# One-hot rows of the slot table in 16 bits, tile innermost, read by the matrix engine at a step of 32 bytes

## The reference

```
xn = layernorm(x)
Q, K, V = spike(layernorm(xn @ W.T + b) * g + beta >= 1)      # three projections, 16 heads of 16
attn = 16 - hamming(Q, K) + log-distance bias                 # 4096 x 4096, never formed: it is linear in Q, K, V
s = spike(layernorm(spike(attn @ V) @ Wo.T + bo))
ids = argmin over 8 centroids of dist2(rmsnorm(xn), centroid) # one expert for each token
y = gated MLP of expert ids[token], 256 -> 2 x 512 -> 256     # a * silu(g), then down
out = x + s * silu(y + xn)
```

## Time and profile before

| | us |
|---|---|
| median of 3 runs | 391.56 (388.51 to 393.59) |
| the profiled execution | 388.83 |
| its span, first to last instruction | 387.0 |
| PE busy | 364.7 (94%) |
| DVE busy | 315.9 (82%) |
| POOL busy | 234.7 (61%) |
| ACT busy | 224.6 (58%) |

### The profile page before, as it was taken

How to read it: one execution, slowest core, us unless ns; L and a number is a source line. 1 busy time by engine, 2 the same in 40 slices (tenths; PEclk the granted TensorE clock), 3 DMA queues, 4 the chain that set the end, 5 groups by cost and what they waited for, 6 DMA issues and landing times.

```text
span 387.0 us, 9389 instructions
## 1 busy us (share of the span) xinstructions
PE 364.7 (94%) x2583; PEld 307.6 (79%) x2584; DVE 315.9 (82%) x785; ACT 224.6 (58%) x611; POOL 234.7 (61%) x296
## 2 busy tenths in 40 slices
PE   8999999999969999985999999999999999999981
PEld 4878888888848888864888888888888888888871
DVE  5989999997688999997578777887877777777873
ACT  5589789888733333444455555555555555555551
POOL 4688777778601444786466666666666666666642
PEclk9999999999999999999899999999999999999998
DMA  6687768463398021539122222223222233321000
GB/s 212 199 303 204 220 180 285 145 180 98 104 207 222 29 83 41 153 96 307 34 72 87 67 67 71 80 86 95 76 81 82 79 95 89 92 78 55 29 16 0
DMA packets 31874, 45.44 MB, mean 117 GB/s; under 512 B 4113, under 2 KB 25810, under 8 KB 31716
## 3 DMA queue, kind: packets, MB, share of 16 engines
q1 hardware_dynamic: 25200, 29.73, 26.2%
q0 software_dynamic: 6416, 15.26, 13.6%
q10 hardware_dynamic: 228, 0.10, 0.1%
HBM read 36.84 MB, written 15.63 MB: 136 GB/s over the span
## 4 chain that ended last, share of the span: by engine, by line
PE 69%; DVE 9%; DMA 8%; issue 7%; ACT 3%; POOL 2%; ACTq 1%; SPq 1%; DVEq 0%; POOLq 0%
PE bank L632 20%; PE bank L450 16%; PE bank L650 10%; PE bank L511 4%; DMA row_a<-rows_a,slot_id 4%; PE bank L615 3%; PE bank L604 2%; DMA down_sb<-in_down_w 2%; PE bank L554 2%; PE bank L429 2%; PE bank L515 2%; ACT d_hi L825 2%; DVE d_lo L1218 1%; PE bank L523 1%; DVE up_lo L1172 1%
## 5 line engine op out<-in xcount | busy, mean ns | idle before, releaser
L1218 DVE TENSOR_TENSOR d_lo<-down_sb,d_hi 128x1024 fp32r<-128x1024 f32 x39 | 47.8, 1226 | 31.7 <-ACT d_hi L825 30.8
L1366 POOL DMA_INDIRECT row_a<-rows_a,slot_id x39 | 41.3, 1060 | 46.8 <-DVE e_o L1232 30.5
L825 ACT ACTIVATE d_hi<-down_sb 128x1024 fp32r x39 | 41.3, 1060 | 41.7 <-issue 26.3
L1399 POOL DMA_INDIRECT out_x<-e_o,slot_id x39 | 44.3, 1137 | 21.0 <-issue 14.5
L632 PE MATMUL bank<-up_hi,e_xh 128*128 x156 | 52.5, 418 | 0.0
L1372 POOL DMA_INDIRECT row_s<-rows_s,slot_id x39 | 39.7, 1018 | 15.6 <-issue 11.6
L632 PE MATMUL bank<-up_lo,e_xh 128*128 x156 | 48.9, 395 | 0.0
L632 PE MATMUL bank<-up_hi,e_xl 128*128 x156 | 48.6, 392 | 0.0
L807 ACT ACTIVATE e_xh<-bank 128x256 fp32r<-128x256 f32 x39 | 15.0, 384 | 40.9 <-PE bank L604 15.2
L753 ACT ACTIVATE junk<-bank 128x256 bf16<-128x256 f32 x96 | 35.4, 378 | 5.1 <-PE bank L450 4.7
L450 PE MATMUL bank<-w_hi,x_hi 128*128 128x264 f32 (+1 forms) x128 | 35.5, 359 | 0.0
(11 more groups left out here) (221 smaller groups left out, 979.2 us busy)
## 6 DMA issues: line engine op xcount, KB each, us to landing
up_raw<-in_up_w SPq DMA_DIRECT2D x16, 512.0 KB, 4.0
rows_a<-xn SPq DMA_DIRECT2D x32, 129.0 KB, 2.4
rows_a<-in_x SPq DMA_DIRECT2D x8, 512.0 KB, 11.6
down_sb<-in_down_w SPq DMA_DIRECT2D x8, 512.0 KB
xs<-in_x SPq DMA_DIRECT2D x7, 512.0 KB, 4.0
rows_s<-s_out SPq DMA_DIRECT2D x8, 256.0 KB, 2.5
blk_tab<-in_blocks SPq DMA_DIRECT2D x1, 1024.0 KB, 5.7
row_a<-rows_a,slot_id POOLq DMA_INDIRECT x39
```

The source lines that it names most:

```text
L825: act.activation(d_hi[:, :, :], down_sb[:, bass.ds(e, 1), :, :].rearrange("p a c n -> p (a c) n"), ACT.Copy).then_inc(d_high, 1)
L1218: V.tensor_tensor(d_lo[:, :, :], down_sb[:, bass.ds(e, 1), :, :].rearrange("p a c n -> p (a c) n"), d_hi[:, :, :].bitcast(F32), ALU.subtra ...
L1366: G.indirect_dma_start(row_a[s % 4][:, :], None, rows_a, bass.IndirectOffsetOnAxis(ap=slot_id[:, s:s + 1], axis=0), bounds_check=N - 1, oo ...
L1399: G.indirect_dma_start(out, bass.IndirectOffsetOnAxis(ap=slot_id[:, s:s + 1], axis=0), e_o[s % 4][:, :], None, bounds_check=N - 1, oob_is_ ...
```

## The change

Everything about the two one-hot tables is kept in 16 bits, and the index of the tile becomes the innermost one. `low_hot` goes from [128, 16, 128] to [128, 128, 16], `high_hot` from [128, 16, 39] to [128, 39, 16], `high_id` from [128, 16, 2, 39] to [128, 2, 39, 16]. The sizes in bytes are the same.

- POOL writes three new tables in 16 bits, between its stage A and its first `norms_out`: `col_of` (2048 elements in each partition, element (s, n) = s), `tile_of_slot` (39 x 16, element (s, n) = s) and `base16` (32 elements). They lie in the place at `at_set`.
- DVE writes the column of each token as 16 bits (`low16`) in place of 32, and a 16-bit copy of its tile (`high16`), one instruction more. In `slot_one_hots` the same four instructions then have only 16-bit operands in SBUF, all with an innermost step of one element. The comparisons read written-out tables, and the vector of 16 tokens' values is repeated along the outer index instead of the inner one.
- DVE waits for the three tables in `positions` and in `slot_one_hots(0)`. ACT waits for both halves of the one-hots before `high_parts(6)`, since that writes over the tables.
- PE's 32 matmuls stand where they stood, but for tile n they take `low_hot[:, :, n]` and `high_id[:, :, :, n]`: 128 and 78 elements of 2 bytes, each 32 bytes behind the one before.

```diff
--- before.py
+++ after.py
@@ -199,10 +199,14 @@
 
         HT = NT // 2
         assert at_xn[3] + 4 * (D + 2) - at_xn[0] >= 2 * HT * P and at_rs[0] - at_ra[2] >= 2 * HT * P
-        low_hot = [place(f"low_hot{q}", [P, HT, P], BF16, at=at)[0] for q, at in enumerate((at_xn[0], at_ra[2]))]
+        low_hot = [place(f"low_hot{q}", [P, P, HT], BF16, at=at)[0] for q, at in enumerate((at_xn[0], at_ra[2]))]
         at_high = (at_thr, at_ra[2] + 2 * HT * P)
-        high_id = [place(f"high_id{q}", [P, HT, 2, ST], BF16, at=at)[0] for q, at in enumerate(at_high)]
-        high_hot, _ = place("high_hot", [P, HT, ST], BF16, at=at_brow)
+        high_id = [place(f"high_id{q}", [P, 2, ST, HT], BF16, at=at)[0] for q, at in enumerate(at_high)]
+        high_hot, _ = place("high_hot", [P, ST, HT], BF16, at=at_brow)
+        col_of, _ = place("col_of", [P, P, HT], BF16, at=at_set)
+        tile_of_slot, _ = place("tile_of_slot", [P, ST, HT], BF16, at=at_set + 2 * P * HT)
+        base16, low16, high16 = (place(name, [P, NT], BF16, at=at_set + 2 * P * HT + 2 * ST * HT + 2 * NT * n)[0]
+                                 for n, name in enumerate(("base16", "low16", "high16")))
         assert 2 * HT * ST <= 6 * D and 4 * HT * ST <= 12 * D
         assert at_high[1] + 4 * HT * ST <= block_arena[0]
         slot_f, _ = place("slot_f", [P, ST], F32)
@@ -252,6 +256,7 @@
             sem("eye_kept"), sem("sgn_made"), sem("lim_made"), sem("lim_put"), sem("fs_rows"), sem("fs_kept"),
             sem("bo_rows"), sem("lim_n"), sem("sq_cen"), sem("cen_split"))
         cols_set, gain_inv = sem("cols_set"), sem("gain_inv")
+        hot_tables = sem("hot_tables")
         ny_kept, bias_n, pick_set = sem("ny_kept"), sem("bias_n"), sem("pick_set")
         sgn = small[:, 0:8]
         tables_made = sem("tables_made")
@@ -586,8 +591,8 @@
             for q in range(2):
                 pe.wait_ge(slot_hot, q + 1)
                 for n in range(HT):
-                    last = pe.matmul(bank[6][:, 0:2 * ST], low_hot[q][:, n, :],
-                                     high_id[q][:, n, :, :].rearrange("p a s -> p (a s)"),
+                    last = pe.matmul(bank[6][:, 0:2 * ST], low_hot[q][:, :, n],
+                                     high_id[q][:, :, :, n].rearrange("p a s -> p (a s)"),
                                      start=(q == 0 and n == 0), stop=(q == 1 and n == HT - 1))
             last.then_inc(slots_summed, 1)
             for k in range(5, NCH):
@@ -781,6 +786,8 @@
             def high_parts(e):
 
                 for half in range(DC):
+                    if e == E - 2 and half == 0:
+                        act.wait_ge(slot_hot, 2)
                     if e == E - 1:
                         act.wait_ge(at_done, DC * NCH // 2 * (half + 1))
                     act.activation(up_hi[:, e, half, :], up_raw[:, e, half, :], ACT.Copy,
@@ -1121,9 +1128,11 @@
                 step(V.tensor_reduce(rt[:, 2, :], A, AX.X, ALU.add))
                 V.tensor_scalar(rt[:, 0, :], rt[:, 2, :], 1.0 / P, 0.5 / P - 0.5, ALU.mult, ALU.add).then_inc(pos_done, 1)
                 dve.wait_ge(pos_done, 1)
+                dve.wait_ge(hot_tables, 3)
                 step(V.tensor_scalar(rt[:, 0, :], rt[:, 0, :], 12582912.0, None, ALU.add))
                 step(V.tensor_scalar(rt[:, 0, :], rt[:, 0, :], -12582912.0, None, ALU.add))
-                step(V.scalar_tensor_tensor(rt[:, 1, :], rt[:, 0, :], -float(P), rt[:, 2, :], ALU.mult, ALU.add))
+                V.tensor_copy(high16[:, :], rt[:, 0, :])
+                step(V.scalar_tensor_tensor(low16[:, :], rt[:, 0, :], -float(P), rt[:, 2, :], ALU.mult, ALU.add))
 
             def tile_experts():
 
@@ -1135,16 +1144,16 @@
             def slot_one_hots(q):
 
                 ts = slice(q * HT, (q + 1) * HT)
-                over_s = lambda m, n: m.unsqueeze(1).broadcast_to([P, HT, n])
-                per_t = lambda m, n: m.unsqueeze(2).broadcast_to([P, HT, n])
+                over_s = lambda m, n: m[:, ts].unsqueeze(1).broadcast_to([P, n, HT])
                 if q == 0:
                     dve.wait_ge(xt_done, NT)
+                    dve.wait_ge(hot_tables, 3)
                     for k in range(4):
                         dve.wait_ge(row_put[k], 16 * NT // 4)
-                V.tensor_tensor(low_hot[q][:, :, :], over_s(col_no[:, :], P), per_t(rt[:, 1, ts], P), ALU.is_equal)
-                step(V.tensor_tensor(high_hot[:, :, :], over_s(tile_no[:, :], ST), per_t(rt[:, 0, ts], ST), ALU.is_equal))
-                V.tensor_tensor(high_id[q][:, :, 0, :], high_hot[:, :, :], per_t(tile_base[:, ts], ST), ALU.mult)
-                step(V.tensor_scalar(high_id[q][:, :, 1, :], high_hot[:, :, :], row_no[:, 0:1], None, ALU.mult))
+                V.tensor_tensor(low_hot[q][:, :, :], col_of[:, :, :], over_s(low16, P), ALU.is_equal)
+                step(V.tensor_tensor(high_hot[:, :, :], tile_of_slot[:, :, :], over_s(high16, ST), ALU.is_equal))
+                V.tensor_tensor(high_id[q][:, 0, :, :], high_hot[:, :, :], over_s(base16, ST), ALU.mult)
+                step(V.tensor_scalar(high_id[q][:, 1, :, :], high_hot[:, :, :], row_no[:, 0:1], None, ALU.mult))
                 dve.sem_inc(slot_hot, 1)
 
             def slot_ids():
@@ -1349,6 +1358,12 @@
                 step_a(k, 0)
 
 
+            iota = lambda table, pattern, base: G.iota(table, pattern, base=base, channel_multiplier=0,
+                                                       allow_small_or_imprecise_dtypes=True).then_inc(hot_tables, 1)
+            iota(col_of[:, :, :], [[1, P], [0, HT]], 0)
+            iota(tile_of_slot[:, :, :], [[1, ST], [0, HT]], 0)
+            iota(base16[:, :], [[P, NT]], -N)
+
             def norms_out(k, i):
                 c = k + 2 * i
                 for pair in range(2):
```

## The result

| | kernel before | changed kernel |
|---|---|---|
| median | 391.56 us (388.51 to 393.59, 5 runs) | 395.98 us (394.87 to 397.25, 5 runs) |
| ratio | | 1.0135, 95% interval 1.0092 to 1.0177 |
| span of the profiled execution | 387.0 us | 393.1 us |

The change costs 1.35%, on 391.56 us 5.3 us with an interval of 3.6 to 6.9. That is clear of noise, though under the 2% that count as slower. The prediction had 392.8 us and a range of 387.5 to 397.7. The sign holds and 395.98 lies in the range, but the loss is twice the 2.6 us that it had, and more than the 4.1 us that its own bounds for the one term allowed.

A forecast was written before the change was run, and what follows sets the result against it. PE was taken to bound the kernel from 114.75 to 155.44 us. To 390.2 us, the middle of four times, it added 2.6 us for PE's reads and 0 for DVE, POOL and ACT: 392.8 us, range 387.5 to 397.7.

The forecast's parts named there:

- the one term: PE's 32 slot-table matmuls reading at a step of 32 bytes: 2.6 us more, 1.6 to 4.1 as the forecast's bounds.
- The bound: From 114.75 to 155.44 us, around the slot table, PE is the bound and DVE is not.
- DVE's instructions: One-hot instructions, each half: first three at 1.217, 0.476 and 0.487 us, fourth unchanged; 3.4 us saved for both halves.
- What reaches PE: nothing: DVE's 3.4 us saving ends in its waits for PE at attention chunks 4 and 5; gain at the end 0.
- POOL and ACT: POOL's three tables take 3.0 us while it is idle; ACT's wait before copying expert 6's weights is free; cost 0.
- PE's step of 32 bytes: Slot-table matmuls on PE, priced by a DVE row, 80 ns more a pair: 2.6 us, passed on to stage C.
- For free: Rival: PE reads the slot table's operands at a step without cost, end stays at 390.2 us; chance 0.27.
- The second: Rival: PE's slot-table reads cost far more, over 2% slower, from 282 ns a pair (7.8 us) on; chance 0.08.
- DVE's saving coming through: Rival: at chunk 4 or 5 the saving reaches the end, 388.8 us, at the utmost 386.8; chance 0.05.
- POOL's tables disturbing DVE: Rival: between 109 and 115 us POOL's writes delay DVE's cast by up to 3.3 us, 396.1 us; chance 0.04.
- The 16-bit forms not running faster: Rival: DVE's one-hot instructions stay as they are and the time is the forecast's; given no chance of its own.

The follow-up runs named there:

- pairs: Changed kernel with the tile outermost again and each token's value written out twice, so PE reads columns side by side; 0.999 of the kernel before.
- step4: Changed kernel with two tiles innermost in place of sixteen, so PE reads both operands at a step of 4 bytes; 389.74 us in one execution.
- high_step: Changed kernel with only the moving operand (high_id) at a step of 32 bytes, low_hot's columns side by side; 1.0128 of the kernel before.
- low_step: Changed kernel with only the stationary operand (low_hot) at a step of 32 bytes, high_id's columns side by side; 1.0046 of the kernel before.
- step16: Changed kernel with eight tiles innermost, so PE reads both operands at a step of 16 bytes; 393.37 us against 388.95 for the kernel before.
- split: Changed kernel with the 32 slot-table matmuls in two lots of 16, the first behind the output projection of chunk 2; 1.0092 of the kernel before.
- four: Kernel before with three more lots of the 32 slot-table matmuls, columns side by side, into an unused part of the bank; 394.46 us against 388.95.

## Why the prediction was right, and where not

1. **The bound.** Right. PE bounds the stretch, and every microsecond added to it came out at the end: 5.2 us in the chain, 5.3 by the ratio.
2. **DVE's instructions.** Right: 1.22, 0.48 and 0.49 us were forecast, 1.213, 0.474 and 0.482 measured.
3. **What reaches PE: nothing.** Right by the trace of `pairs`, with PE's cost taken away; its times leave room for up to 1.8 us. The waits that took the saving up stand where the prediction put them, at chunks 4 and 5; it missed the one at chunk 3 (0.82 us).
4. **POOL and ACT.** Right in effect. The tables took 3.5 us, not 3.0: (2.48 - 0.84) us / 1424 = 1.15 ns an element in place of the 0.95 read off two tiny tables. ACT copied expert 6's weights directly behind its squares and had no wait for the one-hots.
5. **PE's step of 32 bytes.** The direction was right and the size too small: 2.6 us forecast, 3.60 measured, within the 1.6 to 4.1 given. That it came so near is in part luck, since its working was wrong in two ways that partly cancelled. It took the stationary side (80 ns a pair) for the larger; measured, that side adds 25 ns and the moving side 106. And it took DVE's 0.63 ns an element, where PE pays 1.4 ns more for each moving column. An operand of another engine gave the order of size and no more.
6. **What was left out: the clock.** The sum had no term for it. "PE reads slower" was priced with all other matmuls at their old speed, but the slow stretch took 1.61 us more from the 34 matmuls behind it. With the 1.0 us of point 5 this makes the loss twice the forecast: 5.2 us, beyond the 4.1 that the bounds of the one term allowed. The range held because its upper end, 397.7, was laid on the slowest of the four times, 393.59, and so had room for scatter that the clock's term then used. The prediction read the granted clock of 1.00 in the earlier trace rows as a constant of the stretch; in the changed kernel it is 0.50 there for 3.4 us.
7. **The rivals.** "For free" is out, 4.78 us. The second, at over 282 ns a pair, was not reached. DVE's saving coming through: not to be seen in the trace of `pairs`; by its times the whole 3.4 us are out and 1.4 barely in. POOL's tables disturbing DVE: they ended at 110.5, the cast that might have waited began at 111.92 and took 0.29 us as before. The 16-bit forms not running faster: out, 1.213 us for 2.282.

## What to carry to other kernels

Before a layout is turned to suit one engine, ask which engine bounds the stretch and how it will read the new one: here 3.4 us were saved on an engine that waits and 3.6 spent on the one that doesn't. For a moving operand of 16 bits keep at least four columns of each 16 bytes in use, as in `step4`. For DVE's faster form two elements side by side were enough, with the value of each row written out twice, and one was not. And if a change makes PE slower for some microseconds, read the clock behind it as well.

## What the runs showed of the hardware

- PE's moving operand costs 1.8 to 1.9 ns for each new 16 bytes it touches: 143 ns for 78 columns at a step of 32 bytes (`high_step`), and with both operands at a step 149 ns at 32 bytes, 145 at 16, 75 at 8, 38 at 4. The stationary operand costs about a quarter of that, 62 ns for 128 columns at 32 bytes (`low_step`).
- The granted clock can fall behind a stretch in which the trace shows PE busy without a gap: after 4.6 to 4.8 us of pairs at 143 to 149 ns (one profile each of the changed kernel, `high_step` and `step16`), not after 2.4 us of them (`split`, twice), and not after 4.7 us of pairs at 37 ns (`four`).
- DVE's faster form on two 16-bit operands needs no longer run than two elements innermost: 2048 elements took 1.21 to 1.22 us with 16, 8, 4 and 2. With one, a value repeated along the columns, they took 2.28 (`high_step`).
